# Selective scans of a bidirectional state-space layer: the states written over their injections in SBUF for every tile, and GpSimd weighing tiles 0 and 1 as one instruction

## The reference

```
def step(h, ins):
    dt_t, u_t, B_t, C_t = ins
    h = exp(dt_t[..., None] * A) * h + (dt_t * u_t)[..., None] * B_t[:, None, :]
    y_t = einsum('bdn,bn->bd', h, C_t)
    return (h, y_t)
_, ys = scan(step, h0, xs)
y = moveaxis(ys, 0, 1) + u * Dp
y = y * silu(z)
return einsum('bld,ed->ble', y, Wout)
...
x = x + mamba_fwd(xn) + flip(mamba_bwd(flip(xn))) + ffn_and_attention(...)
```

## Time and profile before

| | |
|---|---|
| median of three runs | 1311.38 us (1309.56 to 1317.42) |
| the profiled execution's own time | 1315.2 us |
| its span | 1313.5 us, 18381 instructions |
| DVE busy | 1175.2 us, 89% of the span |
| PE busy | 1038.3 us, 79% |
| ACT busy | 892.6 us, 68% |
| POOL busy | 547.2 us, 42% |
| tail, 970 to 1303 us: DVE, POOL, PE, ACT busy | 320.08, 307.85, 247.32, 205.58 us of 333 |

### The profile page before, as it was taken

The page is one execution under the profiler, slowest core; times in us unless marked ns, Lnnn a source line. Parts: engine busy times, 40 slices in busy tenths (PEclk is TensorE's granted clock), DMA queues, the critical chain, the costliest instruction groups (busy, mean ns, idle before and its releaser), DMA issues. The chain is left out here.

```text
span 1313.5 us, 18381 instructions
## 1 busy us (share of the span) xinstructions
PE 1038.3 (79%) x6017; PEld 340.7 (26%) x6017; DVE 1175.2 (89%) x1728; ACT 892.6 (68%) x1352; POOL 547.2 (42%) x395
## 2 busy tenths in 40 slices
PE   2789996888888888888888888884755977978764
PEld 1443331111111111111111111131411334544311
DVE  7892657999999999999999999838999999999997
ACT  6354558777777777777778887876645667677642
POOL 5030112502332023300000302326779999999896
PEclk9989996999999999999999999995656797787756
DMA  3034332314404464220000010016659676775452
GB/s 102 0 120 160 140 128 84 121 49 114 113 15 127 141 156 134 62 81 29 17 17 21 13 34 18 1 58 154 161 145 246 140 201 165 176 166 146 117 162 62
DMA packets 92386, 134.50 MB, mean 102 GB/s; under 512 B 15060, under 2 KB 45579, under 8 KB 92291
## 3 DMA queue, kind: packets, MB, share of 16 engines
q1 hardware_dynamic: 91266, 131.23, 36.2%
q0 software_dynamic: 1024, 2.10, 0.6%
HBM read 92.75 MB, written 40.24 MB: 101 GB/s over the span
## 5 line engine op out<-in xcount | busy, mean ns | idle before, releaser
L923 DVE TENSOR_REDUCE at_mpart<-psum 128x1 f32<-128x512 f32 x1024 | 637.9, 684 | 44.3 <-PE psum L1104 41.1
L895 ACT ACTIVATE at_probs<-psum 128x1024 f32<-128x1024 f32 x512 | 495.6, 1022 | 142.2 <-PE psum L1134 141.4
L1104 PE MATMUL psum<-at_ks,at_qs 56*128 56x512 bf16 x1024 | 203.0, 393 | 100.1 <-DVE at_mpart L923 99.3
L1147 PE MATMUL psum<-at_probs,at_vg 128*32 128x512 f32 x2048 | 274.8, 609 | 0.7 <-ACT at_probs L895 0.6
L1537 POOL TENSOR_TENSOR t_inject<-shared 128x1024 f32<-128x1024 f32 x92 | 215.5, 2353 | 29.4 <-POOLq L60 19.3
L742 POOL CAST at_m<-at_mneg 128x16 bf16<-128x16 f32 x16 | 4.0, 250 | 483.0 <-DVE at_mneg L928 476.0
L1609 ACT ACTIVATE psum<-shared,aneg 128x512 f32<-128x512 f32 x240 | 164.0, 690 | 51.9 <-DVE t_hc L1738 41.1
L1134 PE MATMUL psum<-at_qs,at_ks 59*128 59x512 bf16 x1024 | 157.4, 380 | 7.4 <-ACT at_probs L895 6.2
L1104 PEld LDWEIGHTS psum<-at_ks,at_qs 56*128 56x128 bf16 x1024 | 49.4, 93 | 424.2 <-DVE at_mpart L923 409.5
L1944 PE MATMUL psum<-t_hc,stack 128*32 128x512 f32 x480 | 94.0, 867 | 74.8 <-POOL t_hc L1522 48.5
L1522 POOL TENSOR_TENSOR t_hc<-t_hp,shared 128x512 f32<-128x512 f32 x100 | 125.9, 1269 | 33.8 <-DVE t_hp L1812 32.6
(11 more groups left out here) (262 smaller groups left out, 1150.1 us busy)
## 6 DMA issues: line engine op xcount, KB each, us to landing
shared<-mp_dt_d SPq DMA_DIRECT2D x64, 256.0 KB, 5.8
mp_ahead_d<-shared SPq DMA_DIRECT2D x7, 2048.0 KB, 7.9
t_ahead<-mp_ahead_d SPq DMA_DIRECT2D x28, 512.0 KB, 4.0
t_w<-in_w SPq DMA_DIRECT2D x46, 256.0 KB
shared<-mp_bc_d SPq DMA_DIRECT2D x152, 64.0 KB, 3.0
shared<-mp_dtu_d SPq DMA_DIRECT2D x36, 256.0 KB, 9.2
shared<-mp_dtu_d SPq DMA_DIRECT2D x56, 128.0 KB, 4.4
mp_u_d<-shared SPq DMA_DIRECT2D x8, 512.0 KB, 4.1
```

What stands on the lines that cost most here:

```text
L895: act.activation(probs[:, u_ % 2, p, :], s_pair[p], ACT.Exp, scale=float(HD) ** -0.5).then_inc(probs_ready, 1)
L923: dve.reduce_max(mpart[:, s % 2, 2 * jp + b, i, kc:kc + 1], ring[x % 3], AX.X).then_inc(ring_free, 1)
L1104: pe.matmul(ring[z_ % 3], qs[half(b, DQ), buf, of_pair(jp, c * CH + i * P, P)], ks[half(b, DQ), buf, of_pair(jp, kc * CH, CH)], start=True ...
L1147: mm = pe.matmul(o_bank[VW * j:VW * (j + 1), :], vg[:, g % 2, kt, j, :], probs[:, u_ % 2, j // 2, CH * (j % 2):CH * (j % 2 + 1)], start=(k ...
```

## The change

Every scan writes its states over its own injection in SBUF, in `inject` or in `ahead`; the decay banks keep only decays, and `hp` is gone. `inject` has eight buffers in place of four. Both engines read the states for the weighing from SBUF. The tile that POOL weighs beside tile 0 is now tile 1, where it was tile 3, and where both are POOL's they are one instruction of 1024 elements (for three tiles: 0 and 1, and 2 by itself); DVE's pair is 2 and 3, where it was 1 and 2. The number of tiles of each engine is the same in every round; POOL's 100 weighings become 70 (30 pairs, 40 single), DVE's stay 90 (50 pairs, 40 single).

The waits move with the buffers: ACT's decay waits only for the scan of tile k-4; POOL's injection waits until the tiles that had its buffers are weighed and their last state kept (`states_read`); SP's load of `ahead` waits for the weighing and keeping of the round, where it waited for its scans.

```diff
-        ND, NI, NHP, NBC, NA = 4, 4, 4, Inputs.NBC, 3
+        ND, NI, NBC, NA, LAG = 4, 8, Inputs.NBC, 3, 3
...
-                return j in (0, 3) or j == 2 and (r < SCATTER or r % 2 == 1)
-            return j == 0 or j == 3 and r % 3 == 1
+                return j < 2 or j == 2 and (r < SCATTER or r % 2 == 1)
+            return j == 0 or j == 1 and r % 3 == 1
...
+        def states(k, n=1):
+
+            if is_ahead(k):
+                x, j = ahead_rounds.index(k // NJ), k % NJ - 2
+                return ahead[:, x % NA, j:j + n, :]
+            x = by_inject[k] % NI
+            return inject[:, x:x + n, :]
...
-                    sp.wait_ge(scanned, NJ * (ahead_rounds[x - NA] + 1) - K0)
+                    done = ahead_rounds[x - NA] + 1
+                    sp.wait_ge(pool_weighed, by_pool[done])
+                    sp.wait_ge(dve_weighed, by_dve[done])
+                    sp.wait_ge(kept, keeps[NJ * done])
...
-                pool.tensor_tensor(hc[:, r % 2, j, :], hp[:, by_pool[k] % NHP, :], cs[:, (NQ * (i // NB) + q) % NBC, :],
-                                   ALU.mult).then_inc(pool_weighed, 1)
+                pool.tensor_tensor(hc[:, r % 2, j:j + n, :], states(k0, n),
+                                   cs[:, (NQ * (i // NB) + q) % NBC, :].unsqueeze(1).to_broadcast([P, n, CH]), ALU.mult)\
+                    .then_inc(pool_weighed, 1)
+
+            def states_read(k):
+
+                for sem_, pool_ in ((pool_weighed, True), (dve_weighed, False)):
+                    parts = [part_of[k_] for k_ in (k, k + 1) if on_pool(k_) == pool_]
+                    if parts:
+                        pool.wait_ge(sem_, parts[-1])
+                if keeps[k + 2]:
+                    pool.wait_ge(kept, keeps[k + 2])
...
-                        pool.wait_ge(scanned, injected_tiles[x - NI + 1] + 1 - K0)
+                        states_read(injected_tiles[x - NI])
...
-                weigh(k - NI + 1)
+                weigh(k - LAG)
...
-                    if on_pool(k - ND):
-                        act.wait_ge(scanned, k - ND + 1 - K0)
-                    else:
-                        act.wait_ge(dve_weighed, part_of[k - ND])
-                    if keeps[k - ND + 1]:
-                        act.wait_ge(kept, keeps[k - ND + 1])
+                    act.wait_ge(scanned, k - ND + 1 - K0)
...
-                dve.tensor_tensor(hc[:, r % 2, j:j + n, :], decays[:, j:j + n, :],
+                dve.tensor_tensor(hc[:, r % 2, j:j + n, :], states(k0, n),
                                   cs[:, m % NBC, :].unsqueeze(1).to_broadcast([P, n, CH]), ALU.mult).then_inc(dve_weighed, 1)
...
-                dve.tensor_tensor_scan(h, decay[k % ND], added,
+                h = states(k)[:, 0, :]
+                dve.tensor_tensor_scan(h, decay[k % ND], h,
                                        last[:, k % PC:k % PC + 1] if n % NCH else 0.0, ALU.mult, ALU.add).then_inc(scanned, 1)
```

More of the change, by code:

```diff
@@ L1252, in on_pool, with groups @@
             if SCATTER <= r < SCATTER + MOVE or GATHER <= r < GATHER + MOVE:
-                return r // NQ in AHEAD and (j == 0 or j == 3 and r % 2 == 1)
+                return r // NQ in AHEAD and (j == 0 or j == 1 and r % 2 == 1)
             if r // NQ in AHEAD:
-                return j in (0, 3) or j == 2 and (r < SCATTER or r % 2 == 1)
-            return j == 0 or j == 3 and r % 3 == 1
[L1258 to L1262, removed]
+                return j < 2 or j == 2 and (r < SCATTER or r % 2 == 1)
+            return j == 0 or j == 1 and r % 3 == 1
+        def groups(r, pool):
+            mine = [on_pool(NJ * r + j) == pool for j in range(NJ)]
+            parts = []
+            for j in (0, 2):
+                parts += [(j, j + 1)] if mine[j] and mine[j + 1] else [(x, x) for x in (j, j + 1) if mine[x]]
+            return parts
         ahead_rounds = [r for r in range(R0, NR) if is_ahead(NJ * r + 2)]
@@ L1268, in tail_stage @@
         injected_tiles = [k for k in range(K0, NK) if not is_ahead(k)]
-        by_pool, keeps = [0], [0]
-        pool_tiles = [k for k in range(K0, NK) if on_pool(k)]
+        keeps = [0]
         for k in range(NK):
-            by_pool.append(by_pool[-1] + (k >= K0 and on_pool(k)))
             keeps.append(keeps[-1] + (k >= K0 and k // PC % NCH < NCH - 1))
-        by_dve, part_of, ends_at = [0], {}, {}
+        by_dve, by_pool, part_of, ends_at = [0], [0], {}, {}
         for r in range(NR):
[L1276 to L1281, removed]
+            for by, pool_ in ((by_dve, False), (by_pool, True)):
+                of_round = groups(r, pool_) if r >= R0 else []
+                for n, (j0, j1) in enumerate(of_round):
+                    ends_at[NJ * r + j1, pool_] = NJ * r + j0
+                    for j in range(j0, j1 + 1):
+                        part_of[NJ * r + j] = by[-1] + n + 1
+                by.append(by[-1] + len(of_round))
         def chunk_at(r, shift):
@@ L1546, in _ @@
                         gather((k - GATHER * NJ) // 2)
-            for k in range(NK - NI + 1, NK):
+            for k in range(NK - LAG, NK):
                 weigh(k)
@@ L1571, in spread_states @@
                     act.wait_ge(injected, by_inject[done])
-                    act.wait_ge(pool_weighed, by_pool[done])
+                    act.wait_ge(pool_weighed, by_pool[done // NJ])
                     act.wait_ge(dve_weighed, by_dve[done // NJ])
@@ L1614, in keep @@
                     return
-                if on_pool(k):
-                    act.wait_ge(scanned, k + 1 - K0)
-                    h = hp[:, by_pool[k] % NHP, :]
-                else:
-                    act.wait_ge(dve_weighed, part_of[k])
-                    h = decay[k % ND]
-                act.activation(last[:, k % PC:k % PC + 1], h[:, CH - 1:CH], ACT.Copy).then_inc(kept, 1)
+                act.wait_ge(scanned, k + 1 - K0)
+                act.activation(last[:, k % PC:k % PC + 1], states(k)[:, 0, CH - 1:CH], ACT.Copy).then_inc(kept, 1)
             def attended(c):
@@ L1798, in _ @@
                     dve.wait_ge(ahead_in[x % NA], 16 * (x // NA + 1))
-                    added = ahead[:, x % NA, j - 2, :]
                 else:
                     dve.wait_ge(injected, by_inject[k + 1])
-                    added = inject[:, by_inject[k] % NI, :]
                 if n % NCH and keeps[k - PC + 1]:
                     dve.wait_ge(kept, keeps[k - PC + 1])
-                if on_pool(k):
-                    h = hp[:, by_pool[k] % NHP, :]
-                    if by_pool[k] >= NHP:
-                        dve.wait_ge(pool_weighed, by_pool[k] - NHP + 1)
-                        dve.wait_ge(kept, keeps[pool_tiles[by_pool[k] - NHP] + 1])
-                else:
-                    h = decay[k % ND]
-                dve.tensor_tensor_scan(h, decay[k % ND], added,
+                h = states(k)[:, 0, :]
+                dve.tensor_tensor_scan(h, decay[k % ND], h,
                                        last[:, k % PC:k % PC + 1] if n % NCH else 0.0, ALU.mult, ALU.add).then_inc(scanned, 1)
```

16 lines of the change are left out of this document (8 added, 8 removed).

## The result

The changed kernel takes 1388.84 us in the median (1386.32 to 1389.54, 4 runs), the one before 1311.71 beside it: a ratio of 1.0577, 95% interval 1.0541 to 1.0613, or 77 us more. The profiled execution shows 74.0 us of it.

What follows compares the result with a forecast made beforehand. DVE was taken to set the tail's pace, POOL 8% behind. 1315.2 + 46 (middle stretch) + 9 (rounds with indirect DMAs) gave 1370 us profiled, 1366 us as median; forecast 1345 to 1395, 8-in-10 range 1328 to 1412.

Steps and rivals of the forecast that it cites:

- Scans at no cost: DVE's 240 scans, now writing SBUF over their input, keep their length: taken 0, bound 2 us.
- POOL's pairs and new waits at no cost: Paired POOL weighings save 5.6 us of POOL's time; its new waits for injection buffers (`states_read`) cost 0.
- The exclusion decides: DVE weighings with two SBUF operands and POOL products each wait for the other's end, less some 0.15 us.
- The signs I named: In the changed profile: pairs near 1.8 us, singles near 1.5, injections over 2353 ns, scans 1.27 us, ACT's L1738 wait gone.
- Middle stretch +46: Rounds 20 to 52: weighings shut out by POOL lengthen each round from 6.45 to 7.9 us, +46 us over 32 rounds.
- my 7.9: The forecast length in us of a middle-stretch round, above a worked mean of 7.7 since some pairs meet an injection too.
- Rounds with the indirect DMAs +9, bounds 0 and +22.6: Rounds 12 to 19 and 56 to 63, 16 pairs and 8 singles: taken +9 us, as DMAs and POOL's free time give room.
- the rival "POOL goes first": POOL goes first whenever it has something ready, so weighings wait longer: +102 us, a median of 1413; chance 0.17.
- ACT's waits taken at 0: DVE's 15.8 us of tail waits for ACT's decays could go: bounds 0 and -15.8, taken 0 as DVE waits elsewhere.
- POOL's floor: Middle stretch: POOL's work plus being shut out needs 7.5 us a round and cannot be quicker, at least +34 us.
- most weighings find a gap: Rival: half the weighing time meets POOL's idle time or indirect DMAs and ACT's waits go, +20 us, 1331; chance 0.12.
- faster: Rival: POOL and weighings run beside one another after all, so the change only removes waits, 1297 us; chance 0.05.

Runs made afterwards that it cites:

- kernel 2: Changed kernel with POOL's injections cut to 8 elements a tile, weighings still reading SBUF: 1308.91 us, ratio 0.997.
- kernel 1: Changed kernel with the states of the tiles DVE weighs back in PSUM and ACT's waits returned, all else as changed: 1313.67 us, ratio 1.0013.
- kernels 1 to 4: kernel 1, kernel 2, kernel 3, and a fourth: changed kernel with only DVE's 40 single weighings reading SBUF, pairs reading PSUM again: 1333.35 us, ratio 1.0164.
- kernel 3: Changed kernel with each POOL injection replaced by four memsets that read nothing, six injection buffers in place of eight: 1317.37 us in one run.
- Kernels 5 and 6: The changed kernel and the kernel before, each without the tail's 32 indirect DMAs and the waits for them: 1361.87 us and 1306.33 us.
- kernel 7: Changed kernel with one more wait: at the start of round 20 POOL waits for DVE's weighing of round 19: 1389.44 us, ratio 1.0594.
- Kernel 8: Changed kernel with POOL waiting in rounds 20 and 21 for the end of its own last instruction before starting the next: 1381.15 us, ratio 1.0513.

## Why the prediction was right, and where it was not

The time is 23 us above the likeliest value and inside the range, by the mechanism that was forecast. By stretches of the profiled executions the forecast and the measured difference are +46 and +49.2 us (rounds 20 to 51), +9 and +25.9 (the rounds with indirect DMAs), 0 and -1.2 (rounds 4 to 11 and 52 to 55).

- **Scans at no cost: right.** 1264 ns; kernel 2 shows it apart from POOL's load.
- **POOL's pairs and new waits at no cost: right** (kernel 1).
- **The exclusion decides: right**, by kernels 1 to 4. The Trainium skill, "SBUF — State Buffer", section "SBUF: two separate sides", has VectorE and GpSimd share an exclusive lock held for the whole instruction, when VectorE has two SBUF inputs and GpSimd reads SBUF. Kernel 1 agrees with the first condition, kernel 3 with the second; the rows show 0.11 to 0.13 us of overlap where the section has none, and the rows count. The signs I named came somewhat stronger: pairs 2.11 us (1.8 said), singles 1.68 (1.5), injections 2495 ns (over 2353). ACT's wait for L1738 is gone.
- **Middle stretch +46, measured +49.2: right in size, partly by luck.** I misread: those scans open rounds 23 and 54, 31 rounds apart. The scan that opens round 20 in the kernel before is this one (timeline of DVE):

```profile
1009.94 1.27 DVE L1812 TENSOR_TENSOR_SCAN t_hp<-psum,last,t_inject 128x512 f32<-128x512 f32 x1
```

  The true pace was 214.45 / 32 = 6.70 us a round, not 6.45, so my 7.9 would have given +38. DVE's list doesn't explain all of it, as I said it did: 7.8 us of the stretch, 0.24 a round, DVE stood idle. The pace now is 8.24 us: 7.98 of it near my 7.9, and 0.26 the one weighing of 9.42 us, which I had in no case.
- **Rounds with the indirect DMAs +9, bounds 0 and +22.6, measured +25.9: the mis-sized term.** The excess of their 24 weighings is 37.3 us with the one of 9.42 us, which falls into the stretch of round 20, and 29.1 without. My upper bound was the length of the 24 weighings, as if each could cost no more than POOL's being shut out by it, 0.94 us on the mean. But DVE sets the pace there too (idle for 0.3 us in rounds 12 to 19), and what a weighing costs it is what is left of POOL's product, up to 2.2 us each: 1.55 us on the mean of the 24. I had also costed an indirect DMA as a gap, from the addition of 0.68 us in the earlier trace rows; for four weighings it was followed by a lost turn instead. Kernels 5 and 6 put the DMAs' part of the whole loss at 77 - 55.5 = 21.5 us. A sign stood in the earlier trace rows: the DVE instruction of 2.68 us was asked for under an indirect DMA's issue (POOL's at 954.41, 1.25 us), and the injection behind the DMA went first. I used the row for the rival "POOL goes first" everywhere; in the changed kernel that holds for these four of the 59 weighings that waited.
- **ACT's waits taken at 0:** 7.1 us of the 15.8 went; a small gain. I also misread as nearly all of DVE's waiting in the tail: it is the scans' line, and from round 4 on DVE stood idle for 30.2 us. And POOL, 92% busy in the earlier trace rows, was 4 points behind DVE, not 8.
- **POOL's floor** of 7.5 us a round was not what set the pace: POOL idled for 1.0 us a round, DVE for 0.1.
- The rival "most weighings find a gap" fell with the pace of 8.24, "faster" with pairs at 2.11 us. "POOL goes first" holds at four places only.

Open: why a weighing asked for under an indirect DMA loses to the injection behind it, and in one case to three more instructions, while in other runs of POOL without a gap it gets in at the first end. The request's own moment doesn't explain it: the one of 9.42 us and the five that ran at once were all asked for in the last 0.11 to 0.15 us of a DMA, and kernel 7's weighing at 1027.72 was asked for under an injection, the third instruction behind the DMA, and lost as well. Kernel 8 shows a remedy at one place, not the cause; gaps everywhere were not tried.

## What to carry to other kernels

Before moving an operand of a VectorE product from PSUM to SBUF, look at what GpSimd does beside it: if it runs products most of the time, each such VectorE instruction waits for the rest of one and then holds up the next. Here the PSUM banks freed earlier took 7.1 us off DVE's waits for ACT, against a loss of 77. Read the mean ns of a shape before and after, not the busy share. When a price depends on which of two engines goes first, price a wait by what can be left of the other engine's instruction, not by the length of one's own. Look at each kind of instruction the other engine can be in, a DMA issue among them, and at what stands behind it. And take a row's round by counting instructions, not by its place in time.

## What the runs showed of the hardware

- A DVE product of two SBUF operands waits for a POOL product's end, less 0.11 to 0.13 us (55 of the 59 that waited in the changed kernel), even between two of POOL's in a row; POOL's next then takes longer by nearly the whole DVE instruction (2.25 us for 1.27; 5.09 for 4.66).
- POOL's memsets don't exclude it: the pair at 1154.33 took 1.20 us beside them. With one operand in PSUM a pair takes 1198 ns beside a busy POOL (kernel 1).
- Asked for under an indirect DMA's issue, weighings ran at once where POOL's weighing stood behind the DMA (five of nine), and lost where an injection did (four). One of these took 9.42 us behind a run of POOL without a gap, and 3.80 us where POOL paused between its instructions (kernel 8).
- The issue of an indirect DMA that starts under such a weighing takes longer. In kernel 3 (memsets) DVE asked at 1004.90, under POOL's pair weighing, was let in at its end and ran until 1008.13; POOL's next DMA took 1.82 us where it takes about 1:

```profile
1004.67 2.37 POOL L1536 TENSOR_TENSOR t_hc<-t_inject,shared 128x1024 f32<-128x1024 f32 x1
...
1007.20 1.82 POOL L1514 DMA_INDIRECT t_rows<-t_x,t_pos  x1 [0.17 <-issue]
```
